# A row pipeline on one core: where the VectorE divides, normalises and quantises

## The reference, cut to what matters

```python
# attention of layer 1 (img part; 16 heads of 16 channels)
q = rms_norm(x @ Wq + bq, gq);  k = rms_norm(ctx @ Wk + bk, gk);  v = ctx @ Wv + bv
probs = softmax(q @ k.T / sqrt(16));  x = x + (probs @ v) @ Wo + bo
# feed forward of layer 1: 4-bit fake quantisation
x_q = clip(round(x / s1), -8, 7);  h = relu(x_q @ W1_q + b1_q)
h_q = clip(round(h / s2), 0, 15);  x = x + h_q @ W2_q + b2_q
```

## Time and profile before

| what | value |
|---|---|
| median of 3 runs | 1391.89 us (1391.68 to 1394.03) |
| profiled execution, its own time | 1390.28 us |
| its span, first to last instruction | 1388.4 us |
| busy share of the span | PE 87%, DVE 52%, ACT 37%, POOL 20% |
| chain that ended last, by engine | PE 64%, DVE 15%, ACT 8%, issue 6%, DMA 4%, POOL 2% |
| mean granted TensorE clock | 0.958 of full |

### The profile page before, as it was taken

The page is one execution under the profiler, slowest core; times in us unless marked ns, Lnnn a source line. Parts: engine busy times, 40 slices in busy tenths (PEclk is TensorE's granted clock), DMA queues, the critical chain, the costliest instruction groups (busy, mean ns, idle before and its releaser), DMA issues.

```text
span 1388.4 us, 20828 instructions
## 1 busy us (share of the span) xinstructions
PE 1207.2 (87%) x7326; PEld 883.5 (64%) x7342; DVE 716.9 (52%) x1680; ACT 514.4 (37%) x1775; POOL 276.9 (20%) x407
## 2 busy tenths in 40 slices
PE   2788876999986877999999999778888888799998
PEld 1445533999973555888888888555555555455555
DVE  5867735212227787544554545556556666333323
ACT  0255551322314565443333333334444544411110
POOL 5444211223223544200000000112112222000000
PEclk9999996999996998999999999898999999999999
DMA  6433208798940600000000002100100000000110
GB/s 186 139 109 109 65 14 320 281 321 326 334 166 8 243 2 1 26 18 1 1 1 1 1 1 92 61 1 1 32 1 1 1 1 1 1 16 16 31 32 30
DMA packets 54235, 103.88 MB, mean 75 GB/s; under 512 B 7692, under 2 KB 38428, under 8 KB 48220
## 3 DMA queue, kind: packets, MB, share of 16 engines
q1 hardware_dynamic: 48884, 95.24, 20.4%
q0 software_dynamic: 2208, 6.03, 1.2%
q10 hardware_dynamic: 3044, 1.33, 0.4%
HBM read 93.96 MB, written 8.43 MB: 74 GB/s over the span
## 4 chain that ended last, share of the span: by engine, by line
PE 64%; DVE 15%; ACT 8%; issue 6%; DMA 4%; POOL 2%; SPq 0%; ACTq 0%; DVEq 0%; POOLq 0%
PE P L2588 8%; PE P L803 6%; PE P L813 5%; PE P L1718 4%; PE P L1763 4%; PE P L1711 4%; PE P L1727 4%; PE P L2599 3%; ACT big L2115 3%; DVE small L440 2%; PE P L1907 2%; PE P L1856 2%; PE P L1862 2%; PE P L1736 2%; PE P L1751 2%
## 5 line engine op out<-in xcount | busy, mean ns | idle before, releaser
L2588 PE MATMUL P<-XNT,big 128*128 128x512 f32 x256 | 112.5, 593 | 0.4 <-DVE small L2635 0.4
L139 POOL TENSOR_TENSOR lrs<-lve,mhalf 128x1 f32<-128x1 f32 x64 | 36.6, 572 | 368.4 <-DVE lve L130 336.9
L440 DVE TENSOR_REDUCE small<-P 128x2 f32<-128x512 f32 x128 | 83.6, 682 | 41.0 <-PE P L288 40.2
L2026 ACT ACTIVATE big<-P,small 128x128 f32<-128x128 f32 x128 | 45.4, 367 | 145.0 <-DVE small L2204 145.0
L842 ACT ACTIVATE big<-P,big 128x128 f32<-128x128 f32 x184 | 52.6, 369 | 124.7 <-PE P L803 124.7
L510 ACT ACTIVATE big<-P 128x512 f32<-128x512 f32 x128 | 72.5, 597 | 63.1 <-PE P L301 58.1
L803 PE MATMUL P<-big 128*128 128x128 f32 x736 | 87.2, 277 | 0.7 <-DMA big<-b_w 0.7
L803 PEld LDWEIGHTS P<-big 128*128 128x128 f32 x736 | 85.2, 194 | 1.3 <-DMA big<-b_w 1.2
L288 PE MATMUL P<-big 90*128 90x256 bf16 x256 | 56.7, 312 | 31.3 <-DMA big<-scr_qk 16.8
L2588 PEld LDWEIGHTS P<-XNT,big 128*128 128x128 f32 x256 | 48.5, 190 | 55.4 <-issue 54.0
L2343 DVE TENSOR_TENSOR big<-P,big 128x512 f32<-128x512 f32 x40 | 27.6, 690 | 108.2 <-ACT big L2083 108.1
(11 more groups left out here) (375 smaller groups left out, 2766.8 us busy)
## 6 DMA issues: line engine op xcount, KB each, us to landing
big<-b_w SPq DMA_DIRECT2D x23, 1028.0 KB, 8.3
big<-b_w SPq DMA_DIRECT2D x23, 1024.0 KB, 6.2
big<-scr_qk SPq DMA_DIRECT2D x96, 96.0 KB
scr_qk<-big SPq DMA_DIRECT2D x8, 384.0 KB
big<-d_w SPq DMA_DIRECT2D x2, 1024.0 KB, 9.8
big<-moe_y SPq DMA_DIRECT2D x8, 256.0 KB, 4.1
big<-e_wq SPq DMA_DIRECT2D x4, 512.0 KB, 5.9
big<-e_wk SPq DMA_DIRECT2D x4, 512.0 KB, 9.5
```

What stands on the lines that cost most here:

```text
L440: dve.tensor_reduce(negM[:, h, :], P[:, h % 2, :].rearrange("p (c s) -> p c s", c=2), AX.X, ALU.max, negate=True).then_inc(a_max, 1)
L2588: m = pe.matmul(P[:, bank, :], w[u][:, k, 128 * c:128 * c + 128], XNT[:, k, 512 * (q % 2):512 * (q % 2) + 512], start=(k == 0), stop=(k == ...
```

## The change

Only the order of DVE's list changes, and only in the pipeline of layer 1. No instruction is added or taken away, no wait is changed and no other engine's list. Before, every step began with the division of the half of the step before it. Now

- in every step the maxima of half w + 1 come first;
- in odd steps `normalise` comes next, then the division of the even half, then `copy_probs`;
- the odd half is divided in its own step, between the two halves of `quantise`, and no longer at the start of the next even step (for the last row: no longer at the start of the following stage).

```diff
             for w in WINDOWS:
                 k, odd = divmod(w, 2)
-                if 0 <= w - 1 < HALVES:
-                    divide(w - 1)
                 if 0 <= w + 1 < HALVES:
                     maxima(w + 1)
+                if odd and 0 <= k + 2 < B:
+                    normalise(k + 2)
+                if odd and 0 <= w - 1 < HALVES:
+                    divide(w - 1)
                 if 0 <= w < HALVES:
                     copy_probs(w)
...
                 else:
-                    if 0 <= k + 2 < B:
-                        normalise(k + 2)
                     if 0 <= k - 2 < B:
                         quantise(k - 2, 0)
+                    if 0 <= w < HALVES:
+                        divide(w)
+                    if 0 <= k - 2 < B:
                         quantise(k - 2, 1)
                 if 2 <= w + 6 < B:
                     routed_row(dve, w + 6)
...
-            divide2(HALVES - 1)
             add2(B - 1)
```

More of the change, by code:

```diff
@@ L1495, in s23_dve @@
                     routed_row(dve, w + 6)
-            return divide, add, quantise, feed, apply
+            return add, quantise, feed, apply
         def s23_pool(pool):
@@ L2188, in s47_dve @@
         def s47_dve(dve, last_rows):
-            divide2, add2, quantise, feed, apply = last_rows
+            add2, quantise, feed, apply = last_rows
             def copy_values4(m):
```

## The result

| | kernel before | changed |
|---|---|---|
| median of 12 runs, us | 1391.05 (1384.77 to 1394.12) | 1383.95 (1379.94 to 1389.63) |
| ratio, 95% interval | | 0.9954 (0.9937 to 0.9972) |
| profiled execution, its time and span | 1390.28, 1388.4 | 1382.04, 1380.2 |
| from the first maxima (L1410, w = -1) to the first product of the next stage on PE | 127.96 | 122.00 |

What follows compares the result with a forecast made beforehand. A loop through DVE's even step, ACT and the second quantisation, no engine being full, bounds the steady pairs; 4.8 + 3.0 + 1.2 = 9.0 us off 1391.89 gives 1382.9 us, eight times in ten 1379.8 to 1388.2.

Steps and rivals of the forecast that it cites:

- The loop: Steady pairs: DVE's even step, ACT and the second quantisation set the period; without the odd half's division 16.62 becomes 15.43 us.
- 4 x 1.19 = 4.8 us for the even steps: Even steps of k = 3, 4, 5 and 6: each period 1.19 us shorter, 4.8 us in all.
- Rival 4: Steady pairs: PE falls to 1.2 GHz, a low pair costs up to 10 us, total about 1402 us; chance 6%.
- `weigh` at A + 4.70, division from A + 5.85: Steady odd step, A being ACT's start of `squares`: odd half's division runs to A + 7.04, 0.33 us to spare.
- the case weighed with the Trainium skill: Steady odd step: POOL's addition blocks two-input `normalise`, DVE slides 0.68 us; sum unchanged if covered, else 1.4 us less.
- The shadow of POOL's L1513: Steady odd step: second L1446 is held until POOL's L1513 ends, so starting up to A + 8.0 costs nothing.
- its own signs: Wrong if odd step's second L1423 waits beyond A + 6.2, L1446 starts after A + 8, period stays over 16, or clock falls.
- The last pairs, 3.0 us: k = 6 and 7: both divisions count, 1.19 + 0.9 + 1.19 - 0.3 = 3.0 us gained.
- The 0.9 for DVE's waits: Last pairs: DVE's waits for `output` and `down`, 0.43 and 0.33, vanish because `output` starts earlier; counted as 0.9 us.
- The first pairs, 1.2 us: k = 1 and 2: earlier `normalise` gains 1.2 us; bounds -0.5, if the routed row's wait is fully paid, and +1.6.
- Nothing behind k = 7: Step of k = 7 and last division: covered by PE's work from about 557 on, so no gain there.
- rival 1: Last two pairs: PE idles less and holds 2.4 GHz, about 2 us more gained, total 1381 us; chance 12%.

Runs made afterwards that it cites:

- the repeat: The changed kernel timed and profiled again with no edit: 1382.54 us, ratio 0.9948 to the kernel before.
- kernel 1: Against the kernel before, only the odd half's division moved, between the two quantisation halves; odd step's front left in old order: 1385.68 us, ratio 0.9965.
- kernel 2: Against the changed kernel, odd half divided at the start of the even step again; only the odd step's front stays reordered: 1387.76 us, ratio 0.9987.
- kernel 6: Changed kernel with PE's transposes of finished rows done four times over the same place: 1380.75 us, ratio 0.9951.
- kernel 5: Changed kernel with POOL's addition to X moved from the odd step's front into the even step: 1385.89 us, ratio 0.998.
- kernel 7: Kernel before, old order, with PE's transposes of finished rows done four times: 1387.62 us, ratio 0.9994.
- 11: Changed kernel with old order up to w = 4, four-fold PE transposes and POOL's addition to X in the even step: 1385.37 us, ratio 0.9972.
- kernel 9: Changed kernel with DVE's order of the kernel before in w = 1 to 4, new order from w = 5 on: 1380.99 us, ratio 0.9949.
- kernel 8: Changed kernel with POOL's addition to X in the even step and four-fold PE transposes: 1381.40 us, ratio 0.9939.
- 10: Changed kernel with old order up to w = 4 and four-fold PE transposes: 1381.05 us, ratio 0.9945.

## Why the prediction was right, point by point

- **The loop.** Right. 5.84 + 0.71 + 7.37 + 1.51 us was forecast at 15.43; pairs at full clock measured 15.37 and, in the repeat, 15.35. Kernels 1 and 2 show that the odd half's division alone does it.
- **4 x 1.19 = 4.8 us for the even steps.** The steps are of the forecast size (1.35 and 1.22), but only two of the four came whole. The windows give 3.58 us. The other two shrank to 0.60 and 0.41 because PE fell to 1.2 GHz from 508 to 515 us. Rival 4's mechanism is real, but it is far cheaper than the 10 us a pair that it was priced at: one low `up`, `weigh` and scores cost 0.64 us in a shorter pair, and the next pair 0.83, since its PE work starts late and DVE waits 0.80 us for the scores (the maxima at 522.22). Kernel 6 shows the same pairs at 15.4 when the clock holds, and kernel 5 shows one at 15.36 in which it falls but `normalise` is not held. (Rival 4's sum starts from 1392.9 where the median was 1391.89, so it gives about 1401 and not 1402.)
- **`weigh` at A + 4.70, division from A + 5.85.** It was A + 5.23 and A + 6.37, because `normalise` was held up by POOL. This is the case weighed with the Trainium skill (SBUF — State Buffer, Who interferes with whom). The trace agrees: two-input L1401 beside L1522 takes 1.33, and 0.88 when the addition is moved (kernel 5). The held time was 0.46, not 0.68. The shadow of POOL's L1513 hid it as forecast in the pairs at full clock. By its own signs the prediction was wrong here in part: L1423 started beyond A + 6.2, and in one steady pair the clock fell, L1446 started after A + 8 and the pair lasted over 16.
- **The last pairs, 3.0 us.** 2.99 measured, and 3.00 in the repeat. The number is the best hit and is luck in part. The two divisions came as forecast: 1.19 + 1.19 - 0.3 = 2.08, and at full clock on both sides it is 14.91 (kernel 7) to 12.85, 2.06 us, of which kernel 1 alone has 1.18 and kernel 2 alone 0.87. The 0.9 for DVE's waits failed as a mechanism: they were to vanish because `output` comes earlier, but kernel 7 is rid of them in the old order. They came from PE at 1.2 GHz (`output` 2.07 us instead of 1.13), and the 0.93 us between 15.84 and 14.91 is the clock. Where it fell there in the new order (kernels 5 to 11 without 7) the window lasted 14.4 and the gain was 1.4.
- **The first pairs, 1.2 us.** This step failed: -1.60 us, below its bound of -0.5. The first window's -0.52 has the sign of the routed row's wait, but lies within that window's scatter; what repeats is the sum of the two (31.71 and 31.69). The walk failed at w = 3, where I took POOL's chain to cover whatever DVE did. The new order puts `normalise`, held up to 1.33 us, and a division ahead of `copy_probs`; PE, which had gone straight on, waits another 1.18 us at `weigh`, and then runs at 1.2 GHz. The maxima of w = 4 are late by 1.08 relative to those of w = 2. With the old order there, kernel 9, this loss is gone (12.52 us again). It is gone as well in the new order where the clock holds, with the same wait of 1.18 us at `weigh` (kernel 6, 12.29; kernel 8, 12.22). So the order brings the wait, and the clock behind it the loss.
- **Nothing behind k = 7.** 0.98 us came there, of rival 1's kind: the granted clock was 1.00 and PE's rows full speed where they had been at 1.2 GHz (0.66). Kernel 2, which has the old place of the last division, needs 9.22 us there at full clock and the changed kernel 9.20, so the last division was covered as forecast.
- **The sum.** -1.60 + 3.58 + 2.99 + 0.98 = 5.95 us in the stage against 9.0 forecast. The 8.2 us between the two spans hold 1.36 us from ahead of the stage and 0.88 from behind it, which the change did not make. The medians differ by 7.1 us. The forecast of 9.0 lies just beyond the interval's 8.8. That the changed kernel's median of 1383.95 came so near to the forecast 1382.9 is luck in part: the kernel before measured 0.8 us less than the 1391.89 it was reckoned from, and 0.98 + 0.93 us of clock in the last windows make up for some of the 2.8 us missed in the first pairs.

## What to carry to other kernels

Read the pipeline's period as a sum of rows round its loop, and look for the one instruction that stands in the loop while the same engine idles just ahead of it; moving that one gives its full length, as 16.61 less 1.19 did here, and moving its neighbours gave nothing in the steady pairs. Before trusting the sum for the short first and last rounds, list what each moved instruction is now queued in front of there: the same order that pays in the steady state put `copy_probs` behind a division in w = 3, made PE wait 1.18 us more, and with the clock's fall behind it cost 1.1 us. When PE's idle time is regrouped, expect its clock to go its own way; compare stage by stage, and only windows at the same granted clock. The hit of 2.99 us in the last window was two thirds the edit and one third the clock, and only a kernel in the old order with a held clock could tell them apart.

## What the runs showed of the hardware that was not expected

- PE's clock fell after waits hardly longer than before. In the steady pairs before, waits of 1.96 and 1.88 us lay 4 us apart and the clock stayed at 1.00; in the changed kernel waits of 2.08 and 0.54 us with `turn` and `up` between them were followed by 1.2 GHz from 508 us on, while the pair ahead, with 1.94 and 0.73, kept full clock. Filling the first of the two with repeated transposes kept it at 1.00 in three steady pairs out of three, in each of four kernels (6, 8, 10, 11). The waits alone don't decide it: behind one wait of 2.25 us in k = 6 the changed kernel kept 1.00, and kernel 9, behind 2.26, fell.
- Useless PE work cost nothing where PE waits: 1.3 us more of it per pair left the kernel before at 16.59 to 16.60 us.
- An instruction with two SBUF inputs on DVE was lengthened by a POOL instruction of 0.73 us that started 0.07 us earlier, from 0.87 to 1.33 us for the pair; the first of the two ended 0.28 us after POOL's, and so did the one-input L1446 beside POOL's 2.04 us at full clock.
